# Layer norms of the main stage without a shift, and its last eight passes written out

## The reference

```
x1 = layernorm(x)                                  # plain, over channels
a  = x1 + delta(layernorm(x1)*g + b)               # a linear attention block:
       q,k,v = split(h @ gates_w + gates_b);  lr = h @ lr_w + lr_b;  k = k/|k|
       A = tril(k k^T, -1) + I;  u = solve(A, v)   # 512x512, lower triangular
       y = (q k^T) (lr * u);  delta = y @ out_w + out_b
f  = a + relu((layernorm(a)*g2 + b2) @ w1 + b1) @ w2 + b2'
x2 = x + f
out = x2 + (silu(n @ wg^T) * (n @ wu^T)) @ wd^T,   n = layernorm(x2)
```

## Time and profile before

| what | us |
|---|---|
| median of 3 runs | 1793.11 |
| lowest, highest | 1792.05, 1793.13 |
| the profiled execution | 1798.49 |
| its span, first to last instruction | 1796.8 |
| TensorE busy | 1713.0 (95%) |
| TensorE weight loads busy | 1549.5 (86%) |
| VectorE, GpSimd, ScalarE busy | 1264.6, 970.2, 760.8 |

### The profile page before, as it was taken

One profiled execution on the slowest core, in us unless ns is written; L12 is line 12 of the kernel. 1 busy time (PEld: TensorE's weight loads), 2 busy tenths in 40 slices (PEclk: granted clock), 3 DMA queues, 4 the chain that ended last, 5 costly groups with the idle time before them and its releaser, 6 DMA issues.

```text
span 1796.8 us, 32849 instructions
## 1 busy us (share of the span) xinstructions
PE 1713.0 (95%) x11682; PEld 1549.5 (86%) x11682; DVE 1264.6 (70%) x2927; ACT 760.8 (42%) x1626; POOL 970.2 (54%) x1269
## 2 busy tenths in 40 slices
PE   5899999579999999999999999999999999999997
PEld 5899999478888889888888888888888899888886
DVE  4677787257777776777777777777776666676664
ACT  4668777123333333333333333333333333333432
POOL 4456775235555555555555555555555555555552
PEclk8999999689999999999999999999999999999999
DMA  4655565311111121111111211111112111111100
GB/s 124 229 194 186 200 209 181 139 40 41 52 53 52 52 76 52 54 59 56 53 53 53 76 52 52 53 52 52 52 53 64 53 51 51 51 53 59 61 16 24
DMA packets 112669, 140.83 MB, mean 78 GB/s; under 512 B 42389, under 2 KB 94872, under 8 KB 112536
## 3 DMA queue, kind: packets, MB, share of 16 engines
q1 hardware_dynamic: 112536, 139.11, 23.5%
HBM read 80.03 MB, written 59.05 MB: 77 GB/s over the span
## 4 chain that ended last, share of the span: by engine, by line
PE 62%; POOL 8%; DVE 6%; issue 4%; ACT 1%; DMA 0%; POOLq 0%; DVEq 0%; ACTq 0%
PE ps L150 29%; PE ps L1002 12%; PE ps L1012 8%; PE ps L917 5%; POOL xn L1447 5%; PE ps L933 4%; PE ps L923 3%; DVE a L1411 2%; POOL sc L1437 2%; DVE bs L1416 1%; POOL ls L1439 1%; DVE mv L1229 1%; DVE hf L1265 1%; ACT sg L1131 1%; POOL sc L1441 0%
## 5 line engine op out<-in xcount | busy, mean ns | idle before, releaser
L1490 POOL TENSOR_TENSOR hl<-hf,hh 128x512 fp32r<-128x512 f32 x128 | 172.6, 1349 | 394.0 <-ACT hh L1136 394.0
L1012 PE MATMUL ps<-wdT,hh 128*128 128x256 f32 x768 | 203.9, 303 | 1.1 <-ACT sg L1131 0.9
L1265 DVE TENSOR_TENSOR hf<-ps,sg 128x512 f32<-128x512 f32 x192 | 132.5, 690 | 88.1 <-PE ps L1002 85.1
L1012 PE MATMUL ps<-wdT,hl 128*128 128x256 f32 x768 | 187.2, 281 | 0.3 <-DVE hl L1270 0.3
L1136 ACT ACTIVATE hh<-hf 128x512 fp32r<-128x512 f32 x192 | 121.4, 632 | 155.1 <-DVE hf L1265 152.0
L1131 ACT ACTIVATE sg<-ps 128x512 f32<-128x512 f32 x192 | 113.6, 592 | 134.3 <-PE ps L1002 134.3
L1002 PE MATMUL ps<-xh3T_hi,wgT 128*128 128x512 f32 x384 | 154.7, 403 | 0.7 <-DVE xh3T_lo L1270 0.7
L1140 ACT ACTIVATE z_hi<-ps 128x256 fp32r<-128x256 f32 x128 | 49.2, 385 | 248.3 <-PE ps L933 246.6
L1002 PE MATMUL ps<-xh3T_lo,wgT 128*128 128x512 f32 x384 | 152.3, 396 | 0.0
L1002 PE MATMUL ps<-xh3T_lo,wuT 128*128 128x512 f32 x384 | 152.0, 396 | 0.0
L1002 PE MATMUL ps<-xh3T_hi,wuT 128*128 128x512 f32 x384 | 151.9, 396 | 0.0
(11 more groups left out here) (223 smaller groups left out, 5818.6 us busy)
## 6 DMA issues: line engine op xcount, KB each, us to landing
gg_scratch<-gg SPq DMA_DIRECT2D x32, 640.0 KB, 3.3
gg<-gg_scratch SPq DMA_DIRECT2D x32, 640.0 KB, 3.8
kx_scratch<-kx SPq DMA_DIRECT2D x32, 522.0 KB, 2.8
kx<-kx_scratch SPq DMA_DIRECT2D x32, 522.0 KB, 3.5
xk<-in_L_attn_x_dram SPq DMA_DIRECT2D x32, 512.0 KB, 4.1
xt<-in_L_attn_x_dram SPq DMA_DIRECT2D x32, 512.0 KB, 4.6
out_dram<-ot SPq DMA_DIRECT2D x32, 512.0 KB, 2.9
low_scratch<-gg SPq DMA_DIRECT2D x128, 16.0 KB, 1.5
```

The source lines that it names most:

```text
L1012: mm = pe.matmul(ps[:, (FG, FU)[j // 2], (j % 2) * C:(j % 2 + 1) * C], part[:, h, blk(j)], wdT[:, h, :], start=(h == 0 and part is hh), st ...
L1265: dve.tensor_tensor(hf[:, h % 2, :], ps[:, up_bank(h), :], sg[:, h % 2, :], ALU.mult).then_inc(hf_ev[h], 1)
L1490: pool.tensor_tensor(hl[:, h, :], hf[:, h % 2, :], hh[:, h, :].bitcast(F32), ALU.subtract).then_inc(hl_ev[h], 1)
```

## The change

Both norms of the main stage compute (a - mean) * scale in the per-token instruction, with the mean read straight from mv2 or mv3. The two GpSimd operations that made the shift go (lines 1439 and 1441). Since VectorE's next statistics overwrite mv2, which GpSimd now reads longer, VectorE waits for xh2_done ahead of them. Waits on `ready` go. `overlapped` writes all 32 passes out.

```
-                    for i in range(NS - GROUP):
-                        body(eng, i, True, i >= 1, i >= 2, i // GROUP, i % GROUP)
-                    with eng.Fori(NS - GROUP, NS) as i:
-                        body(eng, i, True, True, True, None, None)
+                    for i in range(NS):
+                        slot, r = (i // GROUP, i % GROUP) if i < NS - GROUP else (None, None)
+                        body(eng, i, True, i >= 1, i >= 2, slot, r)
                     body(eng, NS, False, True, True, None, None)
                     body(eng, NS + 1, False, False, True, None, None)
...
                 def dve_stats(dve, n_done, bst_, mv_, bns, mvd):
                     for j in range(TB):
-                        dve.wait_ge(ready, 1)
                         dve.wait_ge(bns[j], n_done)
...
-                        op = dve.tensor_scalar(xn[:, j, :], x2[:, j, :], sc3[:, 0, j:j + 1], sc3[:, 1, j:j + 1],
-                                               ALU.mult, ALU.add)
+                        op = dve.tensor_scalar(xn[:, j, :], x2[:, j, :], mv3[:, j, 0:1], sc3[:, j:j + 1],
+                                               ALU.subtract, ALU.mult)
...
+                        after(dve, xh2_done, i)
                         dve_stats(dve, i + 1, bs2, mv2, bn2, mv2_done)
...
-                    pool.tensor_tensor(ls[:, 0, :], mv_[:, :, 1], eps4[:, :], ALU.add).then_inc(steps[0], 1)
-                    pool.wait_ge(steps[0], n_done)
-                    pool.tensor_tensor(sc[:, 0, :], ls[:, 0, :], mhalf4[:, :], ALU.pow).then_inc(steps[1], 1)
-                    pool.wait_ge(steps[1], n_done)
-                    pool.tensor_tensor(ls[:, 1, :], sc[:, 0, :], mv_[:, :, 0], ALU.mult).then_inc(steps[2], 1)
-                    pool.wait_ge(steps[2], n_done)
-                    pool.tensor_tensor(sc[:, 1, :], zero4[:, :], ls[:, 1, :], ALU.subtract).then_inc(done, 1)
-
-                def pool_scale(pool, n_done, dst, src, scale, shift, made):
-                    pool.wait_ge(ready, 1)
+                    pool.tensor_tensor(ls[:, :], mv_[:, :, 1], eps4[:, :], ALU.add).then_inc(plus_eps, 1)
+                    pool.wait_ge(plus_eps, n_done)
+                    pool.tensor_tensor(sc[:, :], ls[:, :], mhalf4[:, :], ALU.pow).then_inc(done, 1)
+
+                def pool_scale(pool, n_done, dst, src, mean, scale, made):
                     pool.wait_ge(made, n_done)
                     for j in range(TB):
-                        op = pool.tensor_scalar(dst[:, j, :], src[:, j, :], scale[:, j:j + 1], shift[:, j:j + 1],
-                                                ALU.mult, ALU.add)
+                        op = pool.tensor_scalar(dst[:, j, :], src[:, j, :], mean[:, j, 0:1], scale[:, j:j + 1],
+                                                ALU.subtract, ALU.mult)
                     return op
...
                 def pool_body(pool, i, att, mlp, down, m, r):
                     if mlp:
                         pool_norm(pool, i, t3_ps, i - 1, mv2, ls2, sc2, l2, mv2_done, ln2_done)
-                        pool_scale(pool, i, xn, a0, sc2[:, 0, :], sc2[:, 1, :], ln2_done).then_inc(xh2_done, 1)
+                        pool_scale(pool, i, xn, a0, mv2, sc2, ln2_done).then_inc(xh2_done, 1)
```

More of the change, by code:

```diff
@@ L828, in delta_block_kernel @@
             shf = mb("shf", [P, TB])
-            bs2, mv2, ls2, sc2 = mb("bs2", [P, TB, 6]), mb("mv2", [P, TB, 2]), mb("ls2", [P, 2, TB]), mb("sc2", [P, 2, TB])
-            bs3, mv3, ls3, sc3 = mb("bs3", [P, TB, 6]), mb("mv3", [P, TB, 2]), mb("ls3", [P, 2, TB]), mb("sc3", [P, 2, TB])
+            bs2, mv2, ls2, sc2 = mb("bs2", [P, TB, 6]), mb("mv2", [P, TB, 2]), mb("ls2", [P, TB]), mb("sc2", [P, TB])
+            bs3, mv3, ls3, sc3 = mb("bs3", [P, TB, 6]), mb("mv3", [P, TB, 2]), mb("ls3", [P, TB]), mb("sc3", [P, TB])
             xn = mb("xn", [P, TB, C])
@@ L863, in delta_block_kernel @@
             y_ps, a0_ev = sems("y_ps", 2), sems("a0_ev", TB)
-            bn2, mv2_done, l2, ln2_done = sems("bn2_", TB), sem("mv2_done"), sems("l2_", 3), sem("ln2_done")
-            bn3, mv3_done, l3, ln3_done = sems("bn3_", TB), sem("mv3_done"), sems("l3_", 3), sem("ln3_done")
+            bn2, mv2_done, l2, ln2_done = sems("bn2_", TB), sem("mv2_done"), sem("l2"), sem("ln2_done")
+            bn3, mv3_done, l3, ln3_done = sems("bn3_", TB), sem("mv3_done"), sem("l3"), sem("ln3_done")
             xhm_done, xh2_done, xh3_done = sem("xhm_done"), sem("xh2_done"), sem("xh3_done")
@@ L889, in after @@
             def after(eng, sem, n, each=1):
-                if isinstance(n, int):
-                    n = min(n, NS)
-                wait(eng, sem, n * each)
+                wait(eng, sem, min(n, NS) * each)
             def overlapped(body):
                 def run(eng):
-                    for i in range(NS - GROUP):
-                        body(eng, i, True, i >= 1, i >= 2, i // GROUP, i % GROUP)
-                    with eng.Fori(NS - GROUP, NS) as i:
-                        body(eng, i, True, True, True, None, None)
+                    for i in range(NS):
+                        slot, r = (i // GROUP, i % GROUP) if i < NS - GROUP else (None, None)
+                        body(eng, i, True, i >= 1, i >= 2, slot, r)
                     body(eng, NS, False, True, True, None, None)
@@ L1427, in _, with pool_norm @@
                     overlapped(dve_body)(dve)
-                def pool_norm(pool, n_done, read, n_read, mv_, ls, sc, steps, mvd, done):
+                def pool_norm(pool, n_done, read, n_read, mv_, ls, sc, plus_eps, mvd, done):
                     for k in range(CB):
```

## The result

The changed kernel takes 1854.6 us (median of 4 runs, 1853.3 to 1856.5) against 1793.1 for the kernel before: a ratio of 1.033, with a 95% interval from 1.032 to 1.035. The forecast was 17 us faster; it came 61.5 us slower (medians).

What follows compares the result with a forecast made beforehand. TensorE, nearly full with 62% of the chain of waits, was taken as the bound, so only its waits could be won: 13.8 + 2.3 + 1.15 = 17.3 us off 1793.1 gives 1776 us, range 1771 to 1787.

Steps and rivals of the forecast that it cites:

- the edits costed at nothing: Main stage: new xn arithmetic, dropped waits on ready, new wait on xh2_done and written-out loop were each counted as 0.
- xn as (a - mean) * scale: GpSimd's xn in the first norm: new arithmetic stays at 0.555 us per instruction, upper bound 0.745.
- Rival 3: GpSimd's xn: subtract-then-multiply costs over 0.16 us more per instruction, so the kernel is slower, 1797 us; chance 0.04.
- Two small operations fewer: GpSimd between power and xn: without L1439 and L1441 xn finishes 0.64 us earlier per pass, saving 13.8 us of TensorE's wait.
- The hold by hl: GpSimd's first xn: VectorE's hl holds it to 1047.54, so 0.66 us of the freed 1.05 counts at its start.
- L933: TensorE's idle time ahead of L933: an earlier CAST and x save 0.23 us in 20 passes, 4.6, counted half, 2.3.
- The last pass: Uncovered chain of the last pass: first norm's xn 0.6 us earlier, second norm's small operations 0.55 less, together 1.15 us.
- Loop, `ready`, xh2_done at nothing: Main stage: writing out the loop, dropping waits on ready and adding the wait on xh2_done were counted as no cost.
- The terms for the wait: TensorE's weight loads waiting for GpSimd's xn, passes 1 to 31: 13.8 us of 14.4 saved, lower end 10.0.

Runs made afterwards that it cites:

- the fast pair: Changed kernel with GpSimd's four xn doing multiply then add instead of subtract then multiply (not a layer norm): 1774.0 us against 1795.2, ratio 0.988.
- the kernel before with the pair: Kernel before with one edit, GpSimd's four xn doing subtract then multiply on the old scalars (not a layer norm): 1901.7 us, one run.

## Why the prediction was wrong

- **The step that failed** is the first of the edits costed at nothing: "xn as (a - mean) * scale". It took 0.555 us, with 0.745 as the upper bound; measured 1.222, that is 0.667 more for each instruction and 2.67 for the four of a pass, against an advance of 0.64. (From the power's end to the last xn's end the pair costs a little less, 5.58 - 3.41 = 2.17, because the holds by VectorE take less of the longer row.) The bound came from the nearest row by size and inputs, an instruction with two input tiles. That row was no bound: it was of another kind of instruction. GpSimd's two-input subtract takes what an addition of its size takes: at 128x1024 the subtract that makes xhm_lo (L1479) has a median of 2.390 us and the addition of L1463 2.384. So of the two kinds of instruction measured only the one with per-token numbers has a dear subtract. The rows had no price for it, and the honest upper end was open.
- **Rival 3** had the mechanism and the point from which it decides (0.16 per instruction), but was priced at its bound, 1797, and given 0.04. What argued it down was that two operations are two operations. The Trainium skill, "GPSIMD Engine Reference", section "3.1 Elementwise", has one rate for bodies of up to two operations per element, and so argued against it as well. The traces do not agree for a subtract (0.926 alone, 1.222 with a multiply); they agree in that the three other pairs cost the same (0.554 to 0.562).
- **Not foreseen at all**: with the longer idle time TensorE's clock falls to its lower level in 13 of passes 2 to 30. TensorE's busy time is 12.0 us longer, beside 46.4 of waiting.
- **Two small operations fewer**: right. With the fast pair TensorE's wait is down to 2.4 us in 2 passes, the first xn lasts 0.88 where 0.9 to 1.0 was said, and passes like those of the loop last 43.1 us instead of 43.6. The hold by hl came as reckoned: 0.88 beside VectorE's hl against 0.554 free. Held to hl's end at 1033.17 the xn would end at 1033.72 at the latest; it ended at 1033.60. That agrees with the Trainium skill ("SBUF — State Buffer", section "SBUF: two separate sides"), by which the one of the two that starts first has the port pair for its whole instruction.
- **L933**: counted 2.3. The idle time fell by 3.1, and all that the passes gained beside the wait for xn is 3.7, with the hold moved to wt. The prediction's 0.23 a pass was 0.15 in most of the passes with a short wait for xn (0.46 to 0.32).
- **The last pass**: the gap ahead of VectorE's xn fell from 2.06 to 1.52, 0.54 where 0.55 was counted. It holds in the changed kernel too:

```profile
1823.63 1.03 POOL L1434 TENSOR_TENSOR sc<-ls,mhalf 128x4 f32<-128x4 f32 x1
...
1824.70 1.38 DVE L1244 TENSOR_SCALAR xn<-x,mv,sc 128x256 f32<-128x256 f32 x4 [1.52 <-POOL sc L1434]
```

- **Loop, `ready`, xh2_done at nothing**: right for the loop (1.001). The wait on xh2_done was not taken away by itself; the expected total without the slow pair leaves it no room. The `ready` waits were only tried together with the loop: there the xn, waited for long, end later by up to 0.15 us.
- **The sum**: 1776 forecast, 1774.0 with the pair replaced. So close a number is in part luck: the kernel before took 2.0 us more on that chip, and the gain is 21.2 against 17.3 counted. The terms for the wait (13.8 counted, 13.7 measured over passes 2 to 30) and for the last pass held, that of L933 was small by about 1.4, and the one that was put at nothing decided the sign.

## What to carry to other kernels

An edit that only swaps the arithmetic of an instruction has a price of its own on each engine: where no row shows that operation on that engine, in that kind of instruction, the upper end is open, and measuring that one instruction settles it before anything is built on it. On GpSimd write x - m with a per-token m as x + (-m), and let an engine with idle time at that place make -m. Where the engine that bounds the kernel starts to wait for each pass, add the clock that it may lose to the wait.

## What the runs showed of the hardware

- GpSimd, 128x256, one input, two per-token numbers: multiply, add 0.554; add, multiply 0.560; multiply, multiply 0.562; subtract, multiply 1.222; multiply, subtract 1.226; subtract alone 0.926. At 128x128: 0.443 for add, multiply, and 0.788 for subtract, multiply. From these two sizes, some 0.33 us and 0.9 ns per element against 0.35 us and 3.4 ns. VectorE's subtract, multiply takes 0.408, as its multiply, add did.
- A short idle time of TensorE's matmuls that comes back in every pass of some 45 us can lower its clock (0.52 for about 3 us behind it) in some passes and not in others that look alike. Of passes 2 to 30, by the wait for xn in each: 0.2 to 0.6 us, none (the kernel before); 0.6 to 1.1, 2 (subtract alone); 1.6 to 2.0, 13 (the changed kernel); 2.5 to 2.9, 22 and 25 (multiply, subtract; the kernel before with the pair). What decides in which passes, the runs don't tell.
